# A gated delta rule attention block: one factor of a block inverse by VectorE transposes instead of TensorE products

## The reference

```python
q, k, v = short_conv(h @ Wq), short_conv(h @ Wk), short_conv(h @ Wv)     # 4 taps, silu
g = exp(-softplus(h @ Wfa @ Wfb + dt_bias) * exp(A_log)); beta = sigmoid(h @ Wb)
def step(S, (qt, kt, vt, gt, bt)):                # scan over T = 1024, per head
    S = S * gt[..., None]
    delta = (vt - einsum('bhk,bhkv->bhv', kt, S)) * bt[..., None]
    S = S + kt[..., None] * delta[:, :, None, :]
    return S, einsum('bhk,bhkv->bhv', qt, S)
x = x + (rmsnorm(o) * norm_w * sigmoid(h @ Wga @ Wgb)) @ Wo
```

## Time and profile before

| | |
|---|---|
| median of 3 runs | 2972.01 us |
| the profiled execution | 2969.01 us, of which its span is 2967.2 us |
| TensorE busy (matmuls) | 2619.1 us, 88% |
| VectorE busy | 2153.5 us, 73% |
| ScalarE, GpSimd busy | 1400.7 us, 1399.0 us, 47% each |
| mean granted TensorE clock | 0.956 of full speed |

### The profile page before, as it was taken

One profiled execution on the slowest core, in us unless ns is written; L12 is line 12 of the kernel. 1 busy time (PEld: TensorE's weight loads), 2 busy tenths in 40 slices (PEclk: granted clock), 3 DMA queues, 4 the chain that ended last, 5 costly groups with the idle time before them and its releaser, 6 DMA issues.

```text
span 2967.2 us, 119848 instructions
## 1 busy us (share of the span) xinstructions
PE 2619.1 (88%) x54704; PEld 1568.7 (53%) x54704; DVE 2153.5 (73%) x3249; ACT 1400.7 (47%) x2586; POOL 1399.0 (47%) x1245
## 2 busy tenths in 40 slices
PE   6799889998999988899988889888978988897889
PEld 3466666666666655665666666666433333332333
DVE  3778777777777767777777777775214999999991
ACT  3445455454554544554544544543326565546342
POOL 0544445444454444444444454443003887867760
PEclk8899999999999999999999999998989999999999
DMA  1000000000000000000000000001001333323330
GB/s 49 21 12 13 14 17 12 15 13 12 19 12 15 12 12 19 12 12 15 12 12 19 12 12 15 12 6 49 1 23 58 111 114 109 114 94 118 114 109 14
DMA packets 52137, 106.71 MB, mean 36 GB/s; under 512 B 7084, under 2 KB 11948, under 8 KB 51376
## 3 DMA queue, kind: packets, MB, share of 16 engines
q1 hardware_dynamic: 51632, 99.04, 10.2%
HBM read 96.65 MB, written 2.37 MB: 33 GB/s over the span
## 4 chain that ended last, share of the span: by engine, by line
PE 62%; DVE 20%; issue 12%; ACT 4%; POOL 1%; DMA 0%; DVEq 0%; SPq 0%; ACTq 0%; POOLq 0%
PE bank L359 9%; PE bank L466 7%; DVE hs L1692 7%; DVE cv L669 6%; PE bank L627 4%; PE bank L394 3%; PE bank L1511 3%; PE bank L424 3%; PE pair L578 3%; PE pair L591 2%; PE bank L531 2%; PE bank L540 2%; PE bank L1433 2%; PE bank L377 2%; PE bank L599 2%
## 5 line engine op out<-in xcount | busy, mean ns | idle before, releaser
L669 DVE SCALAR_TENSOR_TENSOR cv<-raw,taps,cv 128x1024 f32<-128x1024 f32 x288 | 398.6, 1393 | 20.5 <-ACT cv L931 17.9
L1986 POOL TENSOR_TENSOR dBu<-dtu,Bn 128x512 f32<-128x512 f32 x256 | 379.0, 1484 | 53.9 <-DVE hs L1692 53.3
L359 PE MATMUL bank<-xn,W 128*128 128x512 f32 x768 | 381.8, 621 | 0.0
L1511 PE MATMUL bank<-hc,eye 128*128 128x512 f32 x512 | 259.5, 618 | 48.2 <-DVE hc L1698 46.3
L1189 POOL TENSOR_TENSOR kL<-kL,tot 128x512 f32<-128x512 f32 x128 | 179.1, 1399 | 242.7 <-PE bank L424 242.7
L1895 ACT ACTIVATE bank<-dtv,m_A 128x512 f32<-128x512 f32 x256 | 174.9, 689 | 247.1 <-DVE hs L1692 246.8
L1164 POOL TENSOR_TENSOR R<-qn,gate 128x1024 f32<-128x1024 f32 x32 | 108.6, 3392 | 284.6 <-ACT gate L991 284.6
L930 ACT ACTIVATE raw<-bank 128x512 f32<-128x512 f32 x192 | 114.3, 595 | 261.4 <-PE bank L359 259.8
L1698 DVE TENSOR_TENSOR hc<-hs,Cn 128x512 f32<-128x512 f32 x256 | 192.9, 753 | 8.8
L1511 PEld LDWEIGHTS bank<-hc,eye 128*128 128x128 f32 x512 | 91.7, 192 | 202.7 <-DVE hc L1698 128.2
L1191 POOL TENSOR_TENSOR R<-R,tot 128x512 f32<-128x512 f32 x128 | 192.3, 1502 | 0.0
(11 more groups left out here) (270 smaller groups left out, 6040.9 us busy)
## 6 DMA issues: line engine op xcount, KB each, us to landing
Bn<-ssm_rows SPq DMA_DIRECT2D x128, 256.0 KB, 3.5
Cn<-ssm_rows SPq DMA_DIRECT2D x128, 256.0 KB, 3.2
W<-in_head_w SPq DMA_DIRECT2D x32, 448.0 KB, 3.2
WO<-in_out_w SPq DMA_DIRECT2D x32, 192.0 KB, 2.3
xT<-in_xT SPq DMA_DIRECT2D x1, 2048.0 KB, 7.5
out_xT<-xT SPq DMA_DIRECT2D x4, 512.0 KB, 3.7
xn<-in_w_gate SPq DMA_DIRECT2D x1, 1024.0 KB, 5.6
xn<-in_w_up SPq DMA_DIRECT2D x1, 1024.0 KB, 8.7
```

What stands on the lines that cost most here:

```text
L359: m = pe.matmul(psum[bank][:, :], w[:, (kind * KT + k) * P:(kind * KT + k + 1) * P], xn[:, k, b, cols], start=k == 0, stop=k == KT - 1)
L669: dve.scalar_tensor_tensor(cv[m % 2][:, :, :], raw[m % 2][:, :, i:i + SEG], taps[:, h, KQV[n], i:i + 1], cv[m % 2][:, :, :], MUL, ADD).the ...
L1511: pe.matmul(psum[Y_BANKS[jj]][:, :], eye[:, :], hc[(u * ITEMS + i) % AHEAD][:, :], start=False, stop=n == NS - 1, skip_group_check=True).t ...
L1986: pool.tensor_tensor(dBu[at % AHEAD][:, :], dtu[s][:, j, :], Bn[at // DT2 % DEEP][:, :], MUL).then_inc(dBu_set.sem)
```

## The change

- In `inverse` the set dY = Z'Y is gone from TensorE. VectorE subtracts only X -= dX (128x256), then makes Y by its transpose of 32 x 32 blocks of X, with a wait of its own on X between the two. X and Y have a semaphore each (`x_set`, `y_set`). ScalarE's copy of Z waits for Y as well.
- `level` counts two increments per level: GpSimd's L1191 and VectorE's Bc, which now comes behind the merge of Ac. TensorE's next product waits for that one count instead of `diag_set`, `up_q` and `up_k`. The first transpose and the subtractions of levels 1 to 3 in `inverse` wait for the level after them to be counted, in place of TensorE's wait for `bc_set`.
- Waits that another wait implies are dropped on TensorE (in `conv`, `gating`, `turn_v`, `products`, `solved`, `state`, `output`).
- PLACES and the other place lists are drawn anew.

```diff
-                    pe.wait_ge(*diag_set.at(g, li))
                     if li == 0:
-                        pe.wait_ge(*rk_set.at(g))
+                        pe.wait_ge(*diag_set.at(g, 0))
                         pe.wait_ge(*rq_set.at(g))
                     else:
-                        pe.wait_ge(*up_q.at(g, li - 1))
-                        pe.wait_ge(*up_k.at(g, li - 1))
+                        pe.wait_ge(*level.at(g, 2 * li - 1))
                     product(half)
...
                 for li in range(1, NL):
-                    pe.wait_ge(*bc_set.at(g, li))
-                    pe.wait_ge(*xy_set.at(g, li - 1))
-                    blocks(0, Bc[li % 2][:, :, :], X).then_inc(z_made.sem)
+                    pe.wait_ge(*x_set.at(g, li - 1))
+                    blocks(Bc[li % 2][:, :, :], X).then_inc(z_made.sem)
                     yield
                     yield
                     pe.wait_ge(*z_kept.at(g, li - 1))
-                    blocks(0, Y, Z[:, :, :])
-                    blocks(1, Z[:, :, :], Y).then_inc(dxy_full.sem)
+                    blocks(Y, Z[:, :, :]).then_inc(dx_full.sem)
...
-                    dve.tensor_tensor(Bc[li % 2][:, :, :], view[:, :, 0, :], bm[:, li, :, :], MUL).then_inc(bc_set.sem)
                     dve.wait_ge(*diag_set.at(g, li))
                     dve.copy_predicated(Ac[:, :, :], mask(1 + li).bitcast(I32), view[:, :, 1, :]).then_inc(diag_set.sem)
+                    dve.tensor_tensor(Bc[li % 2][:, :, :], view[:, :, 0, :], bm[:, li, :, :], MUL).then_inc(level.sem)
...
+                dve.wait_ge(*level.at(g, 3))
+                dve.transpose(x, y).then_inc(x_set.sem)
                 yield
                 for li in range(1, NL):
                     yield
                     yield
                     yield
-                    dve.wait_ge(*dxy_full.at(g, li - 1))
-                    dve.tensor_tensor(xy, xy, psum[INV][:, :], SUB).then_inc(xy_set.sem)
+                    dve.wait_ge(*dx_full.at(g, li - 1))
+                    if li + 1 < NL:
+                        dve.wait_ge(*level.at(g, 2 * li + 3))
+                    dve.tensor_tensor(x, x, psum[INV][:, 0:NC * SUBB], SUB).then_inc(x_set.sem)
+                    dve.wait_ge(*x_set.at(g, li))
+                    dve.transpose(y, x).then_inc(y_set.sem)
...
                     act.wait_ge(*z_made.at(g, li - 1))
+                    act.wait_ge(*y_set.at(g, li - 1))
                     act.activation(Z[:, :, :], inv_z, ACT.Copy).then_inc(z_kept.sem)
...
                     pool.tensor_tensor(Rv[:, 1, :, 1, :], Rv[:, 1, :, 1, :], spread(two[:, :, 0], 2, half),
-                                       MUL).then_inc(up_q.sem)
+                                       MUL).then_inc(level.sem)
```

Of the places, those of `products` and `inverse` (hundredths of a turn, both stages with lag 1):

```diff
-    (1, [-7.8, -5.8, 2.6, 13, 16.3, 17.1, 27, 30.8, 40.7, 43.6, 53.4, 55.2, 70.5, 73.6, 83.6]),
-    (1, [16.1, 20.3, 21.5, 30.7, 37, 42.2, 42.4, 48.8, 49.4, 56.4, 60.6, 60.6, 64.8, 71.2, 71.2, 74.3, 77.5,
-         78.6, 84.7, 89.9, 90.8]),
+    (1, [0.8, 4.1, 6.9, 15.2, 17.8, 24.6, 31.7, 31.7, 37.9, 46.9, 52.6, 53.3, 67.2, 70.5, 82.3]),
+    (1, [24.9, 28.9, 29.1, 34.9, 35.5, 37.3, 40.6, 48.9, 50.1, 54.1, 55.8, 56.3, 60.4, 67.8, 67.8, 70.4, 70.9,
+         84.5, 84.5, 88.1, 88.1]),
```

More of the change, by code:

```diff
@@ L48 @@
[L48 to L52, removed]
+    (0, [-8.2, 14.4, 26.7, 27.6, 33.5, 34.5]),
+    (0, [27.6, 31.7, 37.1, 47.4, 51, 60.5]),
+    (0, [46.9, 51.8, 55.8, 62.6, 65.1, 65.1]),
+    (0, [67.1, 67.5, 78.1, 100.3]),
+    (0, [62.9, 63.5, 84, 86.2, 89.7, 93.9]),
@@ new lines @@
+    (0, [81.3, 89.6]),
+    (1, [0.8, 4.1, 6.9, 15.2, 17.8, 24.6, 31.7, 31.7, 37.9, 46.9, 52.6, 53.3, 67.2, 70.5, 82.3]),
+    (1, [24.9, 28.9, 29.1, 34.9, 35.5, 37.3, 40.6, 48.9, 50.1, 54.1, 55.8, 56.3, 60.4, 67.8, 67.8, 70.4, 70.9,
+         84.5, 84.5, 88.1, 88.1]),
+    (1, [83.2, 84.6, 85.3, 86.5]),
+    (1, [99.2, 99.2, 106.9]),
+    (2, [10.8, 37.9]),
+    (2, [7.5, 13.7, 17.5, 19.7, 23.3, 28, 31.9, 35.9, 37.3, 47.4, 50.9, 53.2, 55.5, 57.8, 67, 69.4, 72.9,
+         73.7]),
+    (2, [34.2, 44.7, 81.3, 82, 85.1, 85.8, 86.3, 94.4, 105.8, 105.8, 107.2, 111.7, 122.8]),
@@ L60 @@
-FFN_FROM = [0, 0, 43.8, 141.1, 240, 340.5, 429.9, 519.6]
-FRONT_FROM = [-2, 102.3, 199.3, 299.2]
+FRONT_AT = [-11.3, -3.8, -1.2, 10.3, 12.5, 13.1, 13.1, 13.1, 14.6, 16.6, 21.5, 22.2, 24.5, 24.6, 25.8, 25.9, 25.9,
+            26.8, 26.8, 27, 27, 27, 27, 27, 27, 27, 27, 27, 27.3, 34.5, 45.3, 47.2, 54.8, 54.8, 58.6, 59.1, 65.7,
+            74.6, 74.6, 77.9, 82.2, 83.5, 86.1, 89.6]
+FFN_AT = [-22.5, -16.2, -9.4, 5, 18.7, 21, 27, 31.7, 35.6, 36.8, 40.1, 43.6, 48.8, 51.1, 54.4, 57.4, 59, 60.4, 65.7,
+          69.8, 75.3, 77.8, 88.1, 97, 112.9, 206.4]
@@ L62 @@
+FFN_FROM = [0, 0, 52.3, 142.6, 242.7, 342.7, 430.8, 531.5]
+FRONT_FROM = [-3.3, 106.2, 202.1, 303.1]
 EARLY_AT = [
[4 rows of a table removed]
[4 rows of a table added]
 ]
@@ L272, in hybrid_block @@
         rk_set, rq_set = tally("rk_set"), tally("rq_set")
[L273 to L276, removed]
+        bm_set, level, side_set = tally("bm_set"), tally("level", 2 * NL), tally("side_set")
+        up_t, up_l, up_k = tally("up_t", NL), tally("up_l", NL), tally("up_k", NL + 1)
+        up_t1, up_l1, up_q = tally("up_t1"), tally("up_l1"), tally("up_q")
         z_made, z_kept = tally("z_made", NL), tally("z_kept", NL)
-        dxy_full, y_first, xy_set = tally("dxy_full", NL - 1), tally("y_first"), tally("xy_set", NL)
+        dx_full, x_set, y_set = tally("dx_full", NL - 1), tally("x_set", NL), tally("y_set", NL)
         bo_set, off_kept, y64_set = tally("bo_set"), tally("off_kept"), tally("y64_set")
@@ L355, in steps @@
                         bank = take()
-                        if b == 0:
+                        if n == 0 and b == 0:
                             pe.wait_ge(w_loaded[g % 2].sem, 16 * (g // 2 + 1))
@@ L390, in gating @@
                     bank = take()
-                    if b == 0:
-                        pe.wait_ge(w_loaded[g % 2].sem, 16 * (g // 2 + 1))
+                    if h == 0 and b == 0:
                         pe.wait_ge(*hfa_set.at(seg, 1))
@@ L402, in turn_v @@
                     bank = take()
-                    pe.wait_ge(*silued.at(g, 2))
+                    if half == 0:
+                        pe.wait_ge(*silued.at(g, 2))
                     for c in range(4 * half, 4 * half + 4):
@@ L448, in products @@
                     yield
-                pe.wait_ge(*diag_set.at(g, NL))
-                pe.wait_ge(*up_q.at(g, NL - 1))
-                pe.wait_ge(*up_k.at(g, NL - 1))
+                pe.wait_ge(*level.at(g, 2 * NL - 1))
                 for c in range(NC):
@@ L461, in inverse, with blocks @@
                 X, Y = XY[:, 0, :, :], XY[:, 1, :, :]
-                def blocks(at, lhsT, rhs):
+                def blocks(lhsT, rhs):
                     for c in range(NC):
                         for w in range(4):
-                            m = pe.matmul(psum[INV][quad(w), (at * NC + c) * SUBB:(at * NC + c + 1) * SUBB],
-                                          lhsT[quad(w), c, :], rhs[quad(w), c, :])
+                            m = pe.matmul(psum[INV][quad(w), c * SUBB:(c + 1) * SUBB], lhsT[quad(w), c, :], rhs[quad(w), c, :])
                     return m
@@ L482, in inverse @@
                 pe.wait_ge(*bo_set.at(g))
-                pe.wait_ge(*xy_set.at(g, NL - 1))
+                pe.wait_ge(*y_set.at(g, NL - 1))
                 for c in range(NC):
@@ L513, in turn_k @@
                     if q == 0:
-                        pe.wait_ge(*up_q.at(g, NL))
+                        pe.wait_ge(*up_q.at(g))
                     for c in range(4 * q, 4 * q + 4):
@@ L572, in state @@
                         pe.wait_ge(*wT_set.at(g, 1))
-                        if g:
-                            pe.wait_ge(*s_set.at(g - 1, NC - 1))
-                        else:
+                        if g == 0:
                             pe.wait_ge(*s_zeroed.at(0))
@@ L579, in state @@
                     m.then_inc(pred_full.sem)
[L580 to L584, removed]
+                    if c == 4:
+                        pe.wait_ge(*og_set.at(g, 0))
                     for b in range(NB):
@@ L781, in inverse @@
             def inverse(g):
-                xy = XY[:, :, :, :].rearrange("p a c i -> p (a c i)")
+                x, y = (XY[:, i, :, :].rearrange("p c i -> p (c i)") for i in range(2))
                 if g:
@@ L785, in inverse @@
                     dve.wait_ge(*y64_set.at(g - 1))
[L786 to L790, removed]
+                dve.wait_ge(*level.at(g, 1))
+                dve.tensor_tensor(XY[:, 1, :, :], mask(0), Bc[0][:, :, :], SUB).then_inc(y_set.sem)
+                dve.wait_ge(*y_set.at(g, 0))
+                dve.wait_ge(*level.at(g, 3))
+                dve.transpose(x, y).then_inc(x_set.sem)
                 yield
@@ L1216, in inverse @@
                     yield
-                pool.wait_ge(*xy_set.at(g, NL - 1))
```

(1 more changed line is left out.)

17 lines of the change are left out of this document (removed), and 8 rows, old and new, of the table EARLY_AT.

## The result

The changed kernel takes 2776.32 us (median of 4 runs, 2774.31 to 2788.55) against 2970.28 us for the kernel before on the same chip: a ratio of 0.9354, 95% interval 0.9323 to 0.9385, 194 us less. The prediction was 2840 us, 131 us less, with a range of 2770 to 2930.

What follows compares the result with a forecast made beforehand. TensorE's queue was taken to bound the attention. Products -83, blocks -64, clock -16 and new waits +32 sum to -131 us against 2969.0, so 2838, with the median 3.0 above it 2841, stated as 2840 us; range 2770 to 2930.

Steps and rivals of the forecast that it cites:

- What bounds the kernel: Attention goes by TensorE's queue; its idle time, 5.3 us a unit of "issue", comes at borders of instruction blocks.
- The set dY: In `inverse`, four levels x 32 units x 0.65 us leave TensorE: 83 us gained, all on the path.
- second rival: Only the products' own time is saved, TensorE stays starved as before: 2885 to 2950 us, chance 0.18.
- Fewer blocks: TensorE loses two of 12.9 instruction blocks a unit: 2.0 us a unit, 64 us gained; bounds 0 and 5.3 us.
- The clock: Less idle time in TensorE's starved stretch lets the clock fall less often: 0.5 us a unit, 16 us gained.
- VectorE: Transposes and smaller subtractions in `inverse` add 0.71 us of VectorE work a unit, covered; 23 us without that cover.
- The new waits: VectorE's waits on `level` in `inverse` make TensorE's waits grow 1.0 us a unit, 32 us lost; bounds 0 and 3.
- Dropped waits: Waits removed from TensorE gain zero; bounds 0 and a gain of 0.2 us a unit.
- The tail: The 897 us tail keeps its work, only the order is redrawn: zero, with 10 us to either side.
- the forecast's case: Whole kernel at 2840 us by the summed terms, reaching from 2790 to 2885 us; chance 0.60.
- first rival: All of TensorE's starvation goes, "issue" time falls by 4 us a unit: 2735 to 2790 us, chance 0.13.
- The third: Slower, VectorE held by GpSimd at the four waits on `level`, up to 11.6 us a unit: 3030 us, chance 0.06.

Runs made afterwards that it cites:

- The wide products: Changed kernel with two wide products of 256 and 128 columns a level (4 MATMULs) into the unread half bank: 2825.88 us, ratio 0.9422 to the kernel before.
- dY put back: Changed kernel with the 32 products Z'Y of each level back on TensorE, unread, Y still from VectorE: 2995.74 us, ratio 0.9994 to the kernel before.
- the early levels: Changed kernel with the unread products Z'Y back at levels 1 and 2 only: 2864.37 us, ratio 0.9552 to the kernel before.
- the late ones: Changed kernel with the unread products Z'Y back at levels 3 and 4 only: 2917.13 us, ratio 0.9729 to the kernel before.
- Y alone: Kernel before, its places and waits kept, with dY gone from TensorE and Y made by VectorE's transpose: 2802.0 us, ratio 0.9361.
- the two later pairs: Changed kernel beside itself with the kernel before's FRONT_AT, FFN_AT, FFN_FROM, FRONT_FROM, twice: 2795.99 against 2766.98 us, then 2782.46 against 2770.55 us.
- the run without that wait: Changed kernel with the inverse's wait for the level count moved from VectorE to TensorE, new places: 2811.25 us, ratio 0.9389 to the kernel before.

## Why the prediction was right or wrong

- **What bounds the kernel**: right. TensorE's queue bounds the attention before and after, and "issue" is the border of blocks of instructions. The wide products show it from the other side: more array time with few instructions costs a seventh. That the blocks' arrival ends the gaps is seen in the packets' times.
- **The set dY, 83 us, "all on the path"**: the way was right, and the three terms for products, blocks and clock together were too small. They make 163 us; dY put back costs 200 us. In the windows the first and third (2.6 + 0.5 = 3.1 us a unit) measure 3.4 us of busy time, and the second (2.0) measures 2.7. Another way to count comes out nearer: in a stretch that goes at the pace of blocks, two blocks of 3.2 us each are the price, with the array time inside them. My own sentence against the second rival, that every two sets remove a whole block, pointed to it. It is a mean and not a law: one block's worth of sets cost 2.6 us of turn at the early levels (59.2 against 56.7) and 4.2 at the late ones (60.9).
- **Fewer blocks, 2.0 us a unit**: "issue" time fell by 2.7 us. The bound of 0 to 5.3 held it.
- **The clock, 0.5 us a unit**: it rose from 0.96 to 0.98 in the steady part, more than the mean of 0.965 that I named for the span (it was 0.968). The busy time fell by 3.4 us a unit where the sets make 2.6; the other 0.8 us fits the clock, but no run holds the clock alone.
- **VectorE, 0.71 us a unit, covered**: right where it can be read. With old places a unit's VectorE time rose from 46.2 to 47.1 us (1264.70 us in 26.8 units). In the changed kernel it is 46.3 us; why the new order saves it is open.
- **The new waits, 1.0 us a unit, 32 us lost**: wrong. TensorE's waits for other engines stayed at 0.66 us a unit. In the old order they did grow, by 1.3 us, but in a kernel without the waits on `level`, so not by the way that I had priced. I had read the tightest place off the lists and found it short by 0.6 us; in the trace VectorE's subtraction waits 3.5 us for GpSimd in the whole span, three times out of 128, and the first transpose (L772) 2.5 us, once:

```profile
L781 DVE TENSOR_TENSOR XY<-XY,bank x128: 405/409/423, 100.5 to 1868.9; 128x256 f32<-128x256 f32 x128
its engine sat idle before it (us, times) until:
  PE bank L461: 3.8, 9
  POOL R L1178: 3.5, 3
```

  The places are hundredths of a turn and not times. With other work between two steps they are further apart than the places say.
- **Dropped waits, zero**: not contradicted. **The tail, zero with 10 us to either side**: 7 us longer in the first pair of traces, 14 to 15.5 us in the two later pairs, which the lists alone set apart. The sign was not seen, and the margin was too narrow.
- **The rivals.** The result lies at the lower edge of the range, below the forecast's case (2790 to 2885) and inside the first rival's (2735 to 2790). That rival's premise, that all starvation goes, is not what happened: 2.6 us a unit are left. The second, that only the products' own time is saved, is refuted by Y alone (188 us less) and by "issue" time, which halved. The third needed VectorE held by GpSimd; the run without that wait was not faster. The Trainium skill (Runtime: NRT & Kernel Launch, Instruction fetch mechanics) says that crossing a border of blocks is mostly hidden. The traces here differ: 1.84 us of idle time at the border shown above. If it were hidden, products should cost by their array time; here 109 us of wide ones cost 30 us and 83 us of tiny ones 200.

The sum by its own steps, against the 193 us of span: products, blocks and clock -163 put down, -200 by dY back; new waits +32 put down, about 0; tail 0 put down, +7 here. That makes -193; that it meets the span so closely is in part luck, since the -200 was taken on another chip. The forecast missed by 62 us because two errors point the same way: the gain 37 us too small, and a loss of 32 us that did not come; the tail took 7 us back.

## What to carry to other kernels

Where TensorE runs through many tiny products, count its instructions in blocks (here 256, two instructions to a MATMUL with its load) and look whether idle time without a releaser recurs every 128 MATMULs: then the price of a step is near its share of blocks times the time from border to border, and moving it to another engine can be worth more than its own duration (here 6.5 us of turn for 2.6 us of array time). Wide work put among tiny work cost 30 of its 109 us here. Waits for data that stand beside such gaps are not to be added to them: here, where the waits went, the gaps grew by as much. Lists of places that are redrawn for one part should be timed by part: here those of the attention gained nothing that shows by themselves, and those of the tail took 15 us back.

## What the runs showed that was not expected

- Array time can cost less than it lasts: 109 us of wide products added 30 us, while "issue" time fell from 2.8 to 1.8 us a unit, waits for other engines from 0.6 to 0.1, and the clock rose from 0.97 to 0.99.
- A block of instructions costs 3.2 us of turn in the mean (6.5 us for the 512 instructions of dY), and more where the clock falls with it: 135 us for the last two levels against 82 us for the first two.
- The new places lowered TensorE's waits for other engines on the old work (0.7 to 0.2 us a unit, ratio 1.0006) and on the new one (1.7 to 0.5, turn 57.5 us with both), and each time "issue" time rose by about as much (5.3 to 5.8, and 2.0 to 3.2).
